# Cross-attention and a gated low-rank layer on one core: q rotated between the two halves of the maxima, k turned behind the gated z

## The chip, the cores and the metric

The kernel runs on one core of one Trainium2 chip. The metric is the time of one execution on the device, in microseconds (us), taken as the median of several runs. Three runs of the kernel before gave 176.37, 176.38 and 176.39 us.

## What is computed

1024 tokens (16 batches of 64) with 512 numbers each go through two layers with residuals.

```
x = x + xattn(layernorm(x), ctx, ctx, position_ids, Wq, Wk, Wv, Wo)
    q = x Wq (32 heads of 16),  k = ctx Wk,  v = ctx Wv (8 heads of 16, each shared by 4 of q)
    q = q*cos + rotate_half(q)*sin,  k the same
    out = softmax(q k^T / 4) v Wo
x = x + ffn(layernorm(x), A, B, Wq_w, keys)
    gate = softmax over the 16 largest of 64 scores, 0 for the others
    z = x A^T (64 experts of rank 8),  out = (z * gate) B^T * 2
```

## The kernel before

The tokens are worked off in T = 8 tiles of 128 rows. Each of the five engines has its own program, written out by hand; the order of the calls in it is the order of execution, and semaphores join the engines. Nothing is planned by a scheduler.

The middle of the program is `step(i)` for i = 1 to 5, and each step works on four tiles at different stages: the attention of tile i is finished (`turned_scores`, `values`, `project_out`); for n = i + 1 the plain scores are formed, their maxima taken and turned; for p = i + 2 the projections of k, v and q are made and rotated; and from i = 2 on (the code calls this `f >= 0`) tile f = i - 2 goes through the gated layer (`project_down`, `turn_zg`, `up_high`, `up_low`). Before the steps stand `first` and `second`, behind them `last`.

Names and lines that matter here:

- TensorE (PE) multiplies in single precision by three products of parts, high by high, high by low and low by high. `product` (L1044 to L1046) does it for q, chunk by chunk; `high_part` (L1051, L1052) and `low_part` (L1056) for the other projections. `turn` (L1064) transposes a tile in four pieces; `turn_k` (L1085) transposes the rotated k in one piece, `turn_m` (L1120) the maxima in two. `scores` is L1111, `values` L1147, `turned_scores` L1130 and L1136.
- VectorE (DVE): `top(n, 0)` and `top(n, 1)` (L771, two reductions each) take the maxima of the scores of both halves of tile n from the PSUM banks of `ps_s`; `rotate_k(p)` (L730, L732, L737) makes k_r; `rotate_q(p)` (L752 q_a, L754 q_b) reads the q that PE has just projected out of the bank `ps_w0`; `k_low(p)` (L743) splits the turned k, `m_parts(n)` (L781, L783) the maxima, `z_low(f)` (L895) the turned gated z. `residual` is L812, `result` L902.
- GpSimd (POOL): `k_blocks(p, 0)` and `(p, 1)` (L304), then `rotated_q(p)` (L294, q_r = q_a + q_b), then `c_low` (L288). ScalarE (ACT): `k_high` (L478), `z_high` (L549), `o_high` (L507).

What ties the engines around the change:

- `rotate_q(p)` waits on DVE for `q_ps`, which PE signals with the last matmul of `project_q(p, [3])`.
- `up_high(f)` writes the bank `ps_w0` too. PE therefore waits in front of it until `q_rot` says that both halves of `rotate_q(p)` have read the projected q.
- `turn_k(p)` waits on PE for k_r of `rotate_k(p)`. Its output goes on to ACT (`k_high`), DVE (`k_low`) and POOL (`k_blocks`).
- `turn_m(n)` waits for `k_low(p)`, since both transposes use one bank, and for `m_parts(n)`; `up_low(f)` waits for `z_low(f)`.

The wait in front of `up_high`, as PE's `step` has it:

```
pe.wait_ge(v_st_ok, p + 1)
project_out(i)
if f >= 0:
    pe.wait_ge(q_rot, 2 * p + 2)
    up_high(f)
```

Of the kernel before, what the change touches and what calls it, by code (L numbers as in the profile page):

```python
# [51 lines left out]
def build(nc, x, cT, pos, wq, wkv, wo, aT, router, bT, out):  # L52
    ctx = ExitStack()
    with ctx:
# [643 lines left out]
        def _(dve):  # L698
# [5 lines left out]
            def statistics1(t):  # L704
                dve.wait_ge(ld_x[t], 16)
                dve.bn_stats(bn1[:], x_sb[:, t % XN, :]).then_inc(stat1, 1)
                dve.wait_ge(stat1, 3 * t + 1)
                if t >= 2:
                    dve.wait_ge(shift1_ok, t - 1)
                else:  # L710
                    dve.wait_ge(xh_ok, 1)
                dve.bn_aggr(mv1[:], bn1[:]).then_inc(stat1, 1)
                dve.wait_ge(stat1, 3 * t + 2)
                dve.tensor_scalar_add(ve1[:], mv1[:, 1:2], EPS).then_inc(stat1, 1)

            def x_low(t):
                dve.wait_ge(x_hi_ok, t - RAW + 1)
                dve.tensor_tensor(xT_lo[:], xhT_bank(t)[:].rearrange("p (k q) -> p k q", k=DK),
                                  xT_hi[:].bitcast(F32), ALU.subtract).then_inc(x_lo_ok, 1)

            def table(at, t, n):
                return cs[:, t, at:at + HD].rearrange("p (s j) -> p s j", s=2).unsqueeze(1)\
                    .broadcast_to([P, n, 2, J])
# [22 lines left out]
            def rotate_q(t):  # L746
                H = REP * KVH
                dve.wait_ge(q_ps, t + 1)
                if t >= 1:
                    dve.wait_ge(q_r_ok, t)  # L750
                w = ps_w0[:].rearrange("p (h s j) -> p h s j", h=H, s=2)
                dve.tensor_tensor(q_a[:].rearrange("p (h s j) -> p h s j", h=H, s=2), w,  # L752
                                  table(0, t, H), ALU.mult).then_inc(q_rot, 1)
                dve.tensor_tensor(q_b[:].rearrange("p (h s j) -> p h s j", h=H, s=2), w[:, :, ::-1, :],  # L754
                                  table(HD, t, H), ALU.mult).then_inc(q_rot, 1)

            def q_low(t):
                dve.wait_ge(qT_hi_ok, t + 1)
                dve.tensor_tensor(qT_lo[:, t % 2].rearrange("p b r q -> p r b q"),
                                  ps_t0[:].rearrange("p (r b q) -> p r b q", r=REP, b=2),  # L760
                                  qT_hi[:, t % 2].bitcast(F32).rearrange("p b r q -> p r b q"),
                                  ALU.subtract).then_inc(qT_lo_ok, 1)

            def top(t, b):
                dve.wait_ge(s_ps, 2 * t + b + 1)
                if t >= 1 and b == 0:
                    dve.wait_ge(m_lo_ok, t)
                for half in range(2):
                    if b == 0 and half == 1:
                        dve.wait_ge(max_ok, 4 * t + 1)  # L770
                    dve.tensor_reduce(neg_top[:, b, HALF_H * half:HALF_H * (half + 1), :],  # L771
                                      ps_s[:, 2 * (1 - b) + half, :].rearrange("p (r h k) -> p h r k", r=2, h=HALF_H),
                                      AX.X, ALU.max, negate=True).then_inc(max_ok, 1)
# [12 lines left out]
            def attend(t, meanwhile=lambda: None):  # L786
                n = 3 * t
                dve.wait_ge(o_ps, t + 1)
                dve.transpose(o_s[:].rearrange("p h u g d -> p (h u g d)"),  # L789
                              ps_o.rearrange("p h n -> p (h n)")).then_inc(o_step, 1)  # L790
                meanwhile()
                dve.wait_ge(o_step, n + 1)
                for h in range(2):
                    mm = dve.reciprocal(inv[:, h, :], o_s[:, h, :, 1 - h, 0])
                mm.then_inc(o_step, 1)
                dve.wait_ge(o_step, n + 2)
                for h in range(2):
                    mm = dve.tensor_tensor(o_t[:, :, h, :], o_s[:, h, :, h, :],
                                           inv[:, h, :].unsqueeze(2).broadcast_to([P, HD, HD]), ALU.mult)
                mm.then_inc(o_step, 1)  # L800
                dve.wait_ge(o_step, n + 3)
                if t >= 1:
                    dve.wait_ge(oT_lo_ok, t)
                dve.transpose(o_n[:], o_t[:].rearrange("p u g d -> p (u g d)")).then_inc(o_ok, 1)  # L804
# [24 lines left out]
            def x2_low(t):  # L829
                hi, lo = x2T_of(t)  # L830
                dve.wait_ge(x2T_hi_ok, t + 1)
                dve.tensor_tensor(lo[:], x2T_bank(t)[:].rearrange("p (k q) -> p k q", k=DK),  # L832
                                  hi[:].bitcast(F32), ALU.subtract).then_inc(x2T_lo_ok, 1)
# [143 lines left out]
            def step(i):  # L977
                f, g, n, p = i - 2, i - 1, i + 1, i + 2
                if p > RAW:
                    x_low(p)  # L980
                if p + 1 < T:
                    statistics1(p + 1)
                if f >= 0:
                    route(f)
                    x2_low(g)
                attend(i, lambda: q_low(n))
                rotate_k(p)
                if f < 0:
                    x2_low(g)
                top(n, 0)  # L990
                top(n, 1)
                k_low(p)
                if f < 0:
                    m_parts(n)
                rotate_q(p)
                if f >= 0:
                    m_parts(n)
                    z_low(f)
                residual(i)
                statistics2(i)  # L1000
                if f >= 0:
                    result(f)
# [38 lines left out]
        def _(pe):  # L1041
# [41 lines left out]
            def turn_k(t):  # L1083
                pe.wait_ge(k_rot, 3 * t + 3)
                pe.transpose(kT_bank(t), k_r[:], ident[:]).then_inc(kT_ps, 1)  # L1085

            def project_q(t, chunks):
                if t == RAW:
                    pe.wait_ge(wq_l, DK)
                pe.wait_ge(x_hi_ok, t - RAW + 1)  # L1090
                pe.wait_ge(x_lo_ok, t - RAW + 1)
                return product(ps_w0[:], chunk(xT_hi), chunk(xT_lo), wq_hi, wq_lo, slice(0, D), chunks)
# [92 lines left out]
            def turn_zg(t):  # L1185
                pe.wait_ge(zg_ok, t + 1 if t < T - 1 else T + 1)
                turn(ps_t1, zg, DK).then_inc(zT_ps, 1)
# [82 lines left out]
            def step(i):  # L1270
                f, g, n, p = i - 2, i - 1, i + 1, i + 2
                turned_scores(i)
                if f >= 0:
                    pe.wait_ge(x2_ok, i)
                    project_down(f, 0)
                    if f >= 1:
                        pe.wait_ge(res_ok, f)
                    else:
                        pe.wait_ge(q_rot, 2 * p)
                    project_q(p, [0, 1])  # L1280
                    pe.wait_ge(z_ok, 2 * f + 1)
                    project_down(f, 1)
                    turn_x2(g)
                else:
                    pe.wait_ge(q_rot, 2 * p)
                    project_q(p, [0, 1, 2])
                values(i)
                turn_q(n)
                if f < 0:
                    pe.wait_ge(mT_ok, n)  # L1290
                    turn_x2(g)
                if f >= 0:
                    pe.wait_ge(z_ok, 2 * f + 2)
                else:
                    pe.wait_ge(x2_ok, i)
                project_kv(p)
                if f >= 0:
                    project_q(p, [2])
                scores(n, 0)
                scores(n, 1)  # L1300
                if f >= 0:
                    pe.wait_ge(x2T_lo_ok, i)
                    turn_zg(f)
                project_q(p, [3]).then_inc(q_ps, 1)
                turn_k(p)
                pe.wait_ge(v_st_ok, p + 1)
                project_out(i)
                if f >= 0:
                    pe.wait_ge(q_rot, 2 * p + 2)
                    up_high(f)  # L1310
                pe.wait_ge(kT_lo_ok, p + 1)
                turn_m(n)
                if f >= 0:
                    up_low(f)
                if p + 1 < T:
                    if f < 0:
                        pe.wait_ge(x2T_lo_ok, i)
                    turn_xh(p + 1)
# [106 lines left out]
```

## Time and profile before

| | us |
|---|---|
| median of three runs | 176.38 (176.37 to 176.39) |
| the profiled execution's own time | 176.11 |
| its span, first to last instruction | 174.4 |
| PE busy | 168.5 (97% of the span) |
| DVE busy | 132.6 (76%) |
| ACT busy | 90.3 (52%) |
| POOL busy | 85.7 (49%) |

A row of the timeline gives the start and the duration of an instruction (or of several, merged, with their count) in us from the start of the span, then engine, line, operation and its output<-inputs; in brackets stands how long the engine had been idle before it and who ended the idle time. "PE" is the matmul itself, "PEld" the load of its stationary operand, which can run beside the matmul before. Matmuls overlap, so two starts in a row tell more than a duration. The mean granted clock of PE is 1.000 of full speed.

### The profile page before, as it was taken

The page shows a single profiled execution, that of the slowest core. Times are in us where ns is not written, and L with a number is a line of the kernel's source. Part 1 is how long each engine was busy: PE and PEld are TensorE (multiplying, and loading weights), DVE is VectorE, ACT ScalarE, POOL GpSimd, SP SyncE. Part 2 cuts the span into 40 slices and gives each one's busy share as a digit, 9 for nine tenths or more (in the row PEclk, how much of TensorE's full clock was granted, in tenths as well). Part 3 has the DMA queues.
Part 4 walks back from the last instruction along what each step waited for, and adds up shares of the span by engine and source line. Part 5 has one row for each costly group of instructions (what it writes and reads, how often), then busy time and mean ns, then how long its engine had stood idle before and what let it go on. Part 6 is the DMA issues. An engine that isn't in the chain of part 4 may idle for free.

```text
span 174.4 us, 4057 instructions
## 1 busy us (share of the span) xinstructions
PE 168.5 (97%) x1440; PEld 130.3 (75%) x1440; DVE 132.6 (76%) x391; ACT 90.3 (52%) x206; POOL 85.7 (49%) x109
## 2 busy tenths in 40 slices
PE   7999999999989999999999999999999999999994
PEld 2555574677869887888779887888879676889883
DVE  1758857987999899749986699549983998758651
ACT  3578899756468325652647326652527335324210
POOL 5499989599559929122761328103630302421100
DMA  5999911002202020101101000100001001000013
GB/s 169 304 400 389 402 35 62 0 6 60 60 4 60 0 64 0 62 4 29 37 0 60 4 0 0 60 6 0 4 0 60 4 0 60 4 4 0 0 60 120
DMA packets 5332, 11.30 MB, mean 65 GB/s; under 512 B 689, under 2 KB 945, under 8 KB 5057
## 3 DMA queue, kind: packets, MB, share of 16 engines
q1 hardware_dynamic: 5024, 10.79, 17.8%
q10 hardware_dynamic: 288, 0.27, 0.5%
q8 instruction: 11, 0.18, 0.4%
q14 instruction: 9, 0.07, 0.1%
HBM read 8.95 MB, written 2.10 MB: 63 GB/s over the span
## 4 chain that ended last, share of the span: by engine, by line
PE 78%; DVE 8%; ACT 4%; POOL 3%; issue 3%; DMA 2%; ACTq 0%; DVEq 0%
PE ps_w L1051 13%; PE ps_w L1052 12%; PE ps_w L1056 11%; PE ps_t L1064 8%; PE ps_s L1111 6%; PE ps_s L1147 5%; PE ps_s L1130 4%; PE ps_w L1044 3%; PE ps_w L1045 3%; PE ps_w L1046 3%; PE ps_s L1052 2%; PE ps_s L1051 2%; PE ps_s L1056 2%; DMA pos_sb<-pos 2%; POOL wkv_lo L271 2%
## 5 line engine op out<-in xcount | busy, mean ns | idle before, releaser
L313 POOL TENSOR_TENSOR oT_lo<-o_n,oT_hi 128x512 fp32r<-128x512 f32 x8 | 10.3, 1291 | 30.5 <-ACT oT_hi L507 30.5
L771 DVE TENSOR_REDUCE ps_s<-ps_s 128x8 f32<-128x512 f32 x32 | 20.7, 692 | 0.9 <-PE ps_s L1111 0.7
L499 ACT ACTIVATE eT<-ps_s 128x512 f32<-128x512 f32 x32 | 17.0, 599 | 4.1 <-PE ps_s L1136 4.0
L328 POOL TENSOR_TENSOR late<-late,gate 128x512 f32<-128x512 f32 x7 | 7.6, 1082 | 22.2 <-DVE gate L864 22.2
L1051 PE MATMUL ps_w<-am_hi,x2T_hi 128*128 128x288 f32 x48 | 13.9, 312 | 0.0
L1052 PE MATMUL ps_w<-am_lo,x2T_hi 128*128 128x288 f32 x48 | 13.2, 297 | 0.0
L1051 PE MATMUL ps_w<-wo_hi,oT_hi 128*128 128x512 f32 x28 | 11.7, 418 | 0.4 <-ACT oT_hi L507 0.4
L1212 PE MATMUL ps_w<-wq_sb,xT_raw 128*128 128x512 f32 x24 | 11.8, 606 | 0.0
L789 DVE STREAM_TRANSPOSE o_s<-ps_s 128x1024 f32<-128x1024 f32 x8 | 10.0, 1244 | 1.8 <-PE ps_s L1147 1.8
L1051 PE MATMUL ps_w<-b_hi,zT_hi 128*128 128x512 f32 (+1 forms) x28 | 11.2, 406 | 0.0
L507 ACT ACTIVATE oT_hi<-o_n 128x512 fp32r<-128x512 f32 x8 | 5.1, 632 | 11.9 <-DVE o_n L804 11.9
L1052 PE MATMUL ps_w<-wo_lo,oT_hi 128*128 128x512 f32 x28 | 11.1, 396 | 0.0
L1052 PE MATMUL ps_w<-b_lo,zT_hi 128*128 128x512 f32 (+1 forms) x28 | 10.5, 379 | 0.0
L832 DVE TENSOR_TENSOR x2T_lo<-ps_t,x2T_hi 128x512 fp32r<-128x512 f32 x7 | 4.8, 690 | 7.4 <-ACT x2T_hi L520 7.4
L1111 PE MATMUL ps_s<-k_bd_hi,qT_hi 64*128 64x256 f32 x64 | 10.1, 311 | 0.0
L1051 PEld LDWEIGHTS ps_w<-am_hi,x2T_hi 128*128 128x128 f32 x48 | 9.0, 188 | 1.4 <-issue 0.2
L294 POOL TENSOR_TENSOR q_r<-q_a,q_b 128x512 f32<-128x512 f32 x7 | 9.1, 1297 | 2.0 <-DVE q_b L754 2.0
L492 ACT ACTIVATE mT<-ps_t 128x256 fp32r<-128x256 f32 x8 | 3.1, 383 | 13.1 <-PE ps_t L1120 13.1
L304 POOL TENSOR_TENSOR k_bd_lo<-kT_lo,half_mask 128x512 fp32r<-128x512 f32 x8 | 8.8, 1095 | 1.9 <-DVE kT_lo L743 1.9
L1111 PEld LDWEIGHTS ps_s<-k_bd_hi,qT_hi 64*128 64x128 f32 x64 | 6.1, 186 | 4.5 <-issue 4.3
L1111 PE MATMUL ps_s<-k_bd_lo,qT_hi 64*128 64x256 f32 x64 | 9.1, 279 | 0.0
L1111 PE MATMUL ps_s<-k_bd_hi,qT_lo 64*128 64x256 f32 x64 | 9.1, 278 | 0.0
(211 smaller groups left out, 524.6 us busy)
## 6 DMA issues: line engine op xcount, KB each, us to landing
x_sb<-x SPq DMA_DIRECT2D x8, 256.0 KB, 7.4
cT_in<-cT SPq DMA_DIRECT2D x7, 256.0 KB, 3.7
out<-res SPq DMA_DIRECT2D x7, 256.0 KB, 2.0
wq_sb<-wq SPq DMA_DIRECT2D x4, 256.0 KB, 6.4
late<-wo SPq DMA_DIRECT2D x1, 1024.0 KB, 8.6
am_sb<-aT SPq DMA_DIRECT2D x1, 1024.0 KB, 8.8
b_sb<-bT SPq DMA_DIRECT2D x1, 1024.0 KB, 7.4
wkv_sb<-wkv SPq DMA_DIRECT2D x1, 512.0 KB, 4.4
```

The lines of the kernel that those rows point to most:

```text
L294: pool.tensor_tensor(q_r[:].rearrange("p (r k d) -> p k r d", r=REP, k=KVH), q_a[:].rearrange("p (k r d) -> p k r d", r=REP, k=KVH), q_b[: ...
L304: pool.tensor_tensor(bd[:, t % 2], kT[:].bitcast(F32).rearrange("p (b q) -> p b q", b=2).unsqueeze(2) .broadcast_to([P, 2, HALF_H, BATCH]) ...
L313: pool.tensor_tensor(oT_lo[:], o_n[:].rearrange("p (b r q) -> p r b q", b=2, r=REP), oT_hi[:].bitcast(F32), ALU.subtract).then_inc(oT_lo_o ...
L499: act.activation(eT[:, c].rearrange("p b n -> p (b n)"), ps_s[:, c, :], ACT.Exp)\
L771: dve.tensor_reduce(neg_top[:, b, HALF_H * half:HALF_H * (half + 1), :], ps_s[:, 2 * (1 - b) + half, :].rearrange("p (r h k) -> p h r k", ...
L789: dve.transpose(o_s[:].rearrange("p h u g d -> p (h u g d)"), ps_o.rearrange("p h n -> p (h n)")).then_inc(o_step, 1)
L1051: pe.matmul(dst, hi(k), w_hi[:, k, cols], start=(k == 0), stop=False)
L1052: pe.matmul(dst, hi(k), w_lo[:, k, cols], start=False, stop=False)
L1056: mm = pe.matmul(dst, lo(k), w_hi[:, k, cols], start=False, stop=(k == DK - 1))
L1064: mm = pe.transpose(dst[:, P * k:P * (k + 1)], src[:, P * k:P * (k + 1)], ident[:])
L1111: mm = pe.matmul(ps_s[:, 2 * (1 - b) + half, 2 * P * rp:2 * P * (rp + 1)], q[rows, t % 2, b, 2 * rp:2 * rp + 2, :].rearrange("p r q -> p ( ...
L1212: return pe.matmul(ps_w0[:], xT_raw[:, k, :], wq_sb[:, k, :], start=(k == 0), stop=(k == DK - 1))
```

## The change

It moves two calls, in the steps with f >= 0 (i = 2 to 5) alone. On DVE `rotate_q(p)` goes from behind `top(n, 1)` and `k_low(p)` to between `top(n, 0)` and `top(n, 1)`. On PE `turn_k(p)` goes from behind `project_q(p, [3])` to directly behind `turn_zg(f)`, ahead of `project_q(p, [3])`. Step 1, and everything before and behind the steps, keeps its order. Nothing is added or removed, and no wait changes.

```diff
@@ DVE, step(i) @@
                 top(n, 0)
+                if f >= 0:
+                    rotate_q(p)
                 top(n, 1)
                 k_low(p)
                 if f < 0:
                     m_parts(n)
-                rotate_q(p)
-                if f >= 0:
+                    rotate_q(p)
+                else:
                     m_parts(n)
                     z_low(f)
                 residual(i)
@@ PE, step(i) @@
                 if f >= 0:
                     pe.wait_ge(x2T_lo_ok, i)
                     turn_zg(f)
+                    turn_k(p)
                 project_q(p, [3]).then_inc(q_ps, 1)
-                turn_k(p)
+                if f < 0:
+                    turn_k(p)
                 pe.wait_ge(v_st_ok, p + 1)
                 project_out(i)
```

DVE, from the end of `rotate_k(p)` to `m_parts(n)` in one step (four steps have this difference; `kT_lo` is `k_low`, `q_a` and `q_b` are `rotate_q`, the reductions are `top`):

```order
 L737 TENSOR_TENSOR k_r<-ps_w,k_b 128x128
-L771 TENSOR_REDUCE ps_s<-ps_s 128x8 x4
-L743 TENSOR_TENSOR kT_lo<-ps_t,kT_hi 128x128
-L752 TENSOR_TENSOR q_a<-ps_w,cs 128x512
-L754 TENSOR_TENSOR q_b<-ps_w,cs 128x512
+L771 TENSOR_REDUCE ps_s<-ps_s 128x8 x2
+L752 TENSOR_TENSOR q_a<-ps_w,cs 128x512
+L754 TENSOR_TENSOR q_b<-ps_w,cs 128x512
+L771 TENSOR_REDUCE ps_s<-ps_s 128x8 x2
+L743 TENSOR_TENSOR kT_lo<-ps_t,kT_hi 128x128
```

The rotation of q has passed two reductions and `k_low`; those three now stand behind it, and `m_parts` follows at the same place in the sequence.

PE, from the transposes of the gated z to the first matmuls of `project_out`, in a step with f >= 0, before:

```order
L1064 MATMUL ps_t<-ident,late 128x128 x4
L1044 MATMUL ps_w<-wq_hi,xT_hi 128x512
L1045 MATMUL ps_w<-wq_lo,xT_hi 128x512
L1046 MATMUL ps_w<-wq_hi,xT_lo 128x512
L1085 MATMUL ps_t<-ident,k_r 128x128
L1051 MATMUL ps_w<-wo_hi,oT_hi 128x512
L1052 MATMUL ps_w<-wo_lo,oT_hi 128x512
```

and changed, where each of PE's line numbers is two higher because of the two lines that DVE's part has gained:

```order
L1066 MATMUL ps_t<-ident,late 128x128 x4
L1087 MATMUL ps_t<-ident,k_r 128x128
L1046 MATMUL ps_w<-wq_hi,xT_hi 128x512
L1047 MATMUL ps_w<-wq_lo,xT_hi 128x512
L1048 MATMUL ps_w<-wq_hi,xT_lo 128x512
L1053 MATMUL ps_w<-wo_hi,oT_hi 128x512
L1054 MATMUL ps_w<-wo_lo,oT_hi 128x512
```

The transpose of k has passed the three matmuls of the last chunk of q. The text uses the line numbers of the kernel before.

## Rows read from the trace of the kernel before

**Rows 1.** Waits over the whole span, PE's and two of DVE's: total, times, longest
```profile
DVE x2T_lo L832 <- ACT x2T_hi L520: 7.4, 5, 2.5
...
PEld ps_w L1051 <- DVE q_b L754: 1.8, 4, 0.4
...
PE ps_t L1120 <- DVE m_split L783: 0.6, 1, 0.6
...
DVE res L902 <- PE ps_w L1056: 1.8, 4, 0.5
```

**Rows 2.** Busy time by stretch, steps 3 and 4: length, each engine, PEclk
```profile
71.51:91.19 19.68, 19.67 (x181) 16.15 (x181) 15.82 (x48) 10.05 (x23) 8.32 (x9) 1.00 0.10 29
91.19:110.87 19.68, 19.68 (x182) 16.15 (x181) 15.83 (x48) 10.06 (x23) 8.31 (x9) 1.00 0.04 14
```

**Rows 3.** Timeline of step 3, where `project_out` ends and `up_high` begins
```profile
86.21 0.89 PEld L1056 LDWEIGHTS ps_w<-wo_hi,oT_lo 128*128 128x128 f32 x4
86.44 1.10 PE L1056 MATMUL ps_w<-wo_hi,oT_lo 128*128 128x512 f32 x4
86.80 0.68 DVE L754 TENSOR_TENSOR q_b<-ps_w,cs 128x512 f32<-128x512 f32 x1
87.54 0.19 PEld L1051 LDWEIGHTS ps_w<-b_hi,zT_hi 128*128 128x128 f32 x1 [0.44 <-DVE q_b L754]
87.54 0.50 PE L1051 MATMUL ps_w<-b_hi,zT_hi 128*128 128x512 f32 x1
87.88 0.40 PE L1052 MATMUL ps_w<-b_lo,zT_hi 128*128 128x512 f32 x1
88.12 0.40 PE L1051 MATMUL ps_w<-b_hi,zT_hi 128*128 128x512 f32 x1
```

**Rows 4.** Timeline in `last`: `project_out` ends, another projection follows without a wait
```profile
148.69 1.09 PE L1056 MATMUL ps_w<-wo_hi,oT_lo 128*128 128x512 f32 x4
149.62 0.29 PE L1051 MATMUL ps_s<-am_hi,x2T_hi 128*128 128x288 f32 x1
```

**Rows 5.** Timeline of step 3, PE around `turn_zg` and `turn_k`
```profile
83.25 0.66 PE L1064 MATMUL ps_t<-ident,late 128*128 128x128 f32 x4
83.66 0.48 PE L1044 MATMUL ps_w<-wq_hi,xT_hi 128*128 128x512 f32 x1
83.99 0.40 PE L1045 MATMUL ps_w<-wq_lo,xT_hi 128*128 128x512 f32 x1
84.22 0.39 PE L1046 MATMUL ps_w<-wq_hi,xT_lo 128*128 128x512 f32 x1
84.45 0.27 PE L1085 MATMUL ps_t<-ident,k_r 128*128 128x128 f32 x1
84.48 0.48 PE L1051 MATMUL ps_w<-wo_hi,oT_hi 128*128 128x512 f32 x1
84.80 0.40 PE L1052 MATMUL ps_w<-wo_lo,oT_hi 128*128 128x512 f32 x1
```

**Rows 6.** Timeline of step 3, DVE from `rotate_k` to `residual`
```profile
83.27 0.29 DVE L737 TENSOR_TENSOR k_r<-ps_w,k_b 128x128 f32<-128x128 f32 x1
83.48 2.62 DVE L771 TENSOR_REDUCE ps_s<-ps_s 128x8 f32<-128x512 f32 x4
...
84.81 0.69 DVE L771 TENSOR_REDUCE ps_s<-ps_s 128x8 f32<-128x512 f32 x1
...
86.01 0.28 DVE L743 TENSOR_TENSOR kT_lo<-ps_t,kT_hi 128x128 fp32r<-128x128 f32 x1
...
86.21 0.68 DVE L752 TENSOR_TENSOR q_a<-ps_w,cs 128x512 f32<-128x512 f32 x1
...
87.72 0.29 DVE L783 TENSOR_TENSOR m_split<-ps_s,m_split 128x128 fp32r<-128x128 f32 x1
...
87.93 0.68 DVE L895 TENSOR_TENSOR zT_lo<-ps_t,zT_hi 128x512 fp32r<-128x512 f32 x1
```

**Rows 7.** Timeline of step 3, its end: PE's `turn_m` and `up_low`, DVE's `result`
```profile
89.51 0.38 PE L1120 MATMUL ps_t<-ident,m_split 128*128 128x128 f32 x2
...
89.65 1.17 PE L1056 MATMUL ps_w<-b_hi,zT_lo 128*128 128x512 f32 x4
...
90.25 0.15 DVE L827 TENSOR_SCALAR ve<-mv 128x1 f32<-128x1 f32 x1
...
90.86 0.69 DVE L902 TENSOR_TENSOR res<-ps_w,late 128x512 f32<-128x512 f32 x1 [0.45 <-PE ps_w L1056]
```

**Rows 8.** POOL's q_r in step 5, and PE's transposes of it in `last`
```profile
126.92 1.31 POOL L294 TENSOR_TENSOR q_r<-q_a,q_b 128x512 f32<-128x512 f32 x1 [0.16 <-DVE q_b L754]
...
132.94 0.60 PE L1064 MATMUL ps_t<-ident,q_r 128*128 128x128 f32 x4
```

**Rows 9.** Timeline of step 3: what else `project_out` and `up_high` wait for
```profile
83.61 1.29 POOL L313 TENSOR_TENSOR oT_lo<-o_n,oT_hi 128x512 fp32r<-128x512 f32 x1 [3.91 <-ACT oT_hi L507]
...
84.93 0.59 ACT L549 ACTIVATE zT_hi<-ps_t 128x512 fp32r<-128x512 f32 x1
```

## The prediction, on record before the run

> **What bounds the kernel now.** I read the busy shares first, then the waits, then the timeline of one step. PE is busy for 97% of the span. In steps 3 and 4 it is busy for all of their 19.68 us, at the full granted clock, while DVE has about 3.9 us to spare [rows 2]. So the steps are PE's, and an edit that moves no work between engines can gain only what PE loses at a seam. Busy time hides such losses, because the durations overlap and the profile stretches a matmul over a short stall. The list of waits shows them: PE's weight load for `up_high` waits for DVE's q_b four times, 1.8 us in all, once in each step with f >= 0 [rows 1]. That is the wait for the bank in which `rotate_q` reads q. The timeline of step 3 shows it at work: q_b ends at 86.80 + 0.68 = 87.48, and the load starts at 87.54, with no weights fetched beside the matmul before it [rows 3].
>
> **What that wait costs.** Not the 0.44 us of idle weight loading. What counts is the distance of matmul starts. With the wait it is 87.88 - 86.44 = 1.44 us from the first L1056 of `project_out` to the second matmul of `up_high` [rows 3]. Where another projection follows `project_out` without a wait, the four L1056 take 149.62 - 148.69 = 0.93 us [rows 4], and a matmul of 512 columns follows its forerunner by 88.12 - 87.88 = 0.24 us [rows 3], so the clean distance is 1.17 us. The wait costs 1.44 - 1.17 = 0.27 us. The other three steps show the same pattern.
>
> **Part one, the rotation of q moved.** q_a may begin when two reductions are done and q is projected. The third reduction starts at 84.81 today [rows 6], so DVE is free for q_a at about 84.81. The projected q is due from PE: its last matmul starts at 84.22 and ends at 84.61 [rows 5]; part two puts a transpose of 0.10 us ahead of it, which gives 84.71. From a PE end to the DVE start that it releases the trace has 89.65 + 1.17 = 90.82 to 90.86 [rows 7], so 0.04 us, and q is visible at 84.75. That is 0.06 us before DVE wants it. q_a and q_b then take 87.48 - 86.21 = 1.27 us as today [rows 3, 6] and end at 84.81 + 1.27 = 86.08. PE would like to fetch the weights of `up_high` a matmul ahead of its clean start at 86.44 + 0.93 = 87.37, at about 87.14. So q_b is some 1.06 us early and the wait is gone. Gain: 0.27 us per step.
>
> What stands behind the rotation gets later. `k_low` moves from 86.01 to 86.01 + 1.27 = 87.28 and ends at 87.56. The rest of DVE's sequence keeps its start, since the same instructions stand ahead of it: the maxima's parts are ready at 88.01 and zT_lo at 88.61 [rows 6]. PE's `turn_m`, which needs `k_low` and the maxima's parts, starts at 89.51 today [rows 7] and at 89.24 with the gain, 1.2 us after them; `up_low` moves from 89.65 to 89.38, 0.77 us after zT_lo. Both are covered. DVE is done with its statistics at 90.40 and waits for PE with `result` until 90.86 [rows 7]; with PE 0.27 us earlier it waits 0.19 us instead of 0.45. Still PE's.
>
> POOL works in order: the low block of k waits for `k_low` and so starts about 1.3 us later, and q_r and the low part of c move with it. In step 5, q_r ends at 126.92 + 1.31 = 128.23 and PE turns it at 132.94 [rows 8]; 1.3 us later still leaves over 3 us. In the other steps the same transpose comes in the next step, further away. These delays cost nothing. If that cover were gone, each would be worth up to 1.3 us.
>
> **Part two, k turned behind the gated z.** PE issues the same transpose at another place. Alone behind the q chunk it costs (84.80 - 84.22) - 2 x 0.235 = 0.11 us, counting the slow start of the matmul behind it; 0.235 because undisturbed starts lie 0.23 or 0.24 apart [rows 3, 5]. As the fifth of a run it costs one more spacing, (83.66 - 83.25) / 4 = 0.10 us [rows 5]. The difference is 0.01 us a step, and I take nothing. The good bound is that the slow exit from the lone transpose (84.80 - 84.48 = 0.32 against 0.235, so 0.09 us) is saved in full and the fifth transpose of the run adds nothing: 4 x 0.09 = 0.36 us. The bad one is a wait: k_r ends at 83.27 + 0.29 = 83.56 [rows 6], and the transpose would start at 83.66. With the 0.06 us from q_b's end to the load behind it [rows 3], k_r is visible at 83.62; the margin is 0.04 us, and if the weight load is held, up to 0.1 us more is lost in a step, 0.4 us in all. A slip of the last q chunk by that much would also make DVE wait by 0.1 us, inside its slack. I take zero, because both ends are small and the exact times say that it just fits.
>
> The Trainium skill, in "TensorE: Matmul & The Clock Gate", section "Back-to-back issue gap", gives about 81 ns per matmul for a sustained stream of weight loads and matmuls of 128 columns. By that the fifth transpose would cost 0.08 us instead of 0.10, and the sum would gain 4 x 0.02 = 0.08 us more. The row here says 0.10.
>
> ACT gets the turned k about 0.8 us sooner, and with it zT_hi, both used later than they are ready. No DMA is moved.
>
> **The sum.** 4 x 0.27 = 1.08 us off, nothing added. The profiled execution's own time is 176.11 us and its span 174.4; they would become 175.03 and 173.3. The median of the runs lies 0.27 us above the profiled one, so I forecast 176.38 - 1.08 = **175.30 us**. `last` waits only for work that the steps before it hand over, so it moves forward as a whole.
>
> **The rivals.** About 0.2% (0.35 us) is what a measurement of this kernel can tell from no change.
>
> *Also the transposes pay.* The lone transpose's slow exit is saved fully: 1.08 + 0.36 = 1.44 us, so 174.94. For it: two exits in rows 5 cost 0.09 each, and one of them disappears. Against it: the single transpose itself shows almost no spacing of its own (84.45 to 84.48), so the exit is the price that it has today. Chance 0.12.
>
> *DVE held by q.* `rotate_q` now waits for the last chunk of q with two reductions, `k_low`, `m_parts` and `z_low` behind it. Were the chunk late by more than the 0.77 us that `up_low` has in hand, PE would wait there instead and the gain would shrink towards nothing. At 0.77 + 0.27 = 1.04 us the time would be today's, 176.4. Against it stands that the chunk comes 0.06 us early and that PE and DVE start this stretch from the same event, the values of tile i. Chance 0.07, with the case that another wait takes the place of q_b's at `up_high`; oT_lo (ready at 84.90) and zT_hi (85.52) are both over 1 us early [rows 9].
> The same page of the Trainium skill says, in the section on the 16 small arrays, that VectorE works off its queue in strict order while TensorE may fetch weights ahead. By that rule nothing behind `rotate_q` can pass it; the trace here has no case with `rotate_q` in this place.
>
> *PE held by k, slower than before.* The transpose of k now stands in front of the last q chunk and of `project_out`. If k_r came later than today relative to PE, PE would stand still. The point from which it decides is 0.04 us of margin plus the 0.27 us gained. If one more operation of 128x512 got ahead of k_r on DVE (0.59 us, q_a to q_b), PE would lose 0.55 us and gain 0.27: 4 x 0.28 = 1.1 us more, 177.5. Against it: nothing on DVE ahead of `rotate_k` has changed, and DVE idles for x2T_hi ahead of the attention, 7.4 us in five times [rows 1], so no delay is carried over. Chance 0.04.
>
> *It does nothing that can be measured*, since small losses of k's wait and the reduction order eat most of the gain. That needs 0.73 us of losses; the bounds above give 0.4. Chance 0.03.
>
> **Chances and range.** My forecast, 175.3 with its own bounds of 174.9 to 175.7, has 0.74. Faster by over 0.2%: 0.74 + 0.12 = 0.86. Within 0.2%: most of the DVE case and the last, 0.09. Slower: 0.05. The range goes from just under the transposes' case, 174.85, to the bad bound of k's wait (175.30 + 0.4 = 175.7) and a little into the shrunken gains, 175.95.
>
> **What would show it.** Right: PE's wait for q_b is missing from the waits, the distance from the first L1056 of `project_out` to the second matmul of `up_high` is 1.17 us in the four steps, a step takes 19.4 us instead of 19.68, the low block of k starts some 1.3 us later, and DVE has no wait before q_a over 0.1 us. Wrong: a wait of PE for k_r before the transpose, a wait of DVE for the projected q that reaches `z_low`, a new wait of PE at `turn_m` or `up_low`, or a longer `last`.

## The result, and the profile after

The changed kernel takes 175.18 us in the median of nine runs, beside 176.32 us for the kernel before. The ratio, taken over all runs and not from the two medians (their quotient is 0.9935), is 0.9945, with a 95% interval of 0.9924 to 0.9966: 0.34% to 0.76% faster. The forecast was 175.30. Two further sets of runs of the same kernel, beside the kernel before on the same chip, gave 175.13 us (ratio 0.9928, 0.9906 to 0.9950) and 175.25 us (0.9934, 0.9913 to 0.9955).

| | before | after |
|---|---|---|
| median | 176.32 us | 175.18 us |
| span of the profiled execution | 174.4 us | 173.3 us |
| its own time | 176.11 us | 174.97 us |
| PE busy | 168.5 us | 167.6 us |
| DVE busy | 132.6 us | 132.6 us |

First the waits. These are whole-span rows of the changed kernel (total, times, longest). PE's line numbers are two higher than before.

```profile
POOL k_bd_lo L304 <- DVE kT_lo L743: 7.7, 5, 1.7
...
DVE res L902 <- PE ps_w L1058: 0.7, 4, 0.2
...
PE ps_t L1122 <- DVE m_split L783: 0.6, 1, 0.6
```

PE's wait for q_b [rows 1] is no longer in the list, and no wait of PE in the steps has come in its place. The wait of DVE's `result` for PE has shrunk from 1.8 to 0.7 us: with PE earlier, DVE's slack there is nearly used up. POOL now waits for the late `k_low`.

The stretches from one start of `turned_scores` to the next, for steps 3 and 4 of the changed kernel, answer to [rows 2]:

```profile
71.16:90.56 19.40, 19.40 (x180) 16.25 (x179) 15.82 (x48) 10.05 (x23) 8.21 (x10) 1.00 0.09 30
90.56:109.97 19.41, 19.41 (x181) 16.27 (x180) 15.83 (x48) 10.06 (x23) 8.23 (x10) 1.00 0.04 14
```

A step has gone from 19.68 to 19.40 us. The seam between `project_out` and `up_high` in step 3, in the changed kernel's timeline, answers to [rows 3]:

```profile
85.06 0.68 DVE L754 TENSOR_TENSOR q_b<-ps_w,cs 128x512 f32<-128x512 f32 x1
...
86.06 1.09 PE L1058 MATMUL ps_w<-wo_hi,oT_lo 128*128 128x512 f32 x4
86.77 0.19 PEld L1053 LDWEIGHTS ps_w<-b_hi,zT_hi 128*128 128x128 f32 x1
...
87.00 0.40 PE L1053 MATMUL ps_w<-b_hi,zT_hi 128*128 128x512 f32 x1
...
87.23 0.40 PE L1054 MATMUL ps_w<-b_lo,zT_hi 128*128 128x512 f32 x1
```

q_b ends at 85.74, and PE fetches the weights of `up_high` at 86.77, 0.23 us ahead of their matmul at 87.00. From the first low matmul of `project_out` to the second of `up_high` it is 87.23 - 86.06 = 1.17 us, where it was 1.44.

PE around the moved transpose, in the same timeline, answers to [rows 5]:

```profile
82.90 0.66 PE L1066 MATMUL ps_t<-ident,late 128*128 128x128 f32 x4
...
82.93 0.29 DVE L737 TENSOR_TENSOR k_r<-ps_w,k_b 128x128 f32<-128x128 f32 x1
...
83.28 0.14 PEld L1087 LDWEIGHTS ps_t<-ident,k_r 128*128 128x128 f32 x1
83.39 0.27 PE L1087 MATMUL ps_t<-ident,k_r 128*128 128x128 f32 x1
...
83.42 0.48 PE L1046 MATMUL ps_w<-wq_hi,xT_hi 128*128 128x512 f32 x1
...
84.20 0.40 PE L1053 MATMUL ps_w<-wo_hi,oT_hi 128*128 128x512 f32 x1
...
84.43 0.39 PE L1054 MATMUL ps_w<-wo_lo,oT_hi 128*128 128x512 f32 x1
```

From the first transpose to the second matmul of `project_out` it is 1.53 us, where it was 84.80 - 83.25 = 1.55. The rows show why so little comes of it. The fifth transpose of the run costs 0.11 us: from the first transpose to the q chunk it is 83.42 - 82.90 = 0.52 us, where it was 83.66 - 83.25 = 0.41. What the lone transpose had cost behind the chunk is saved: 0.03 us to the first matmul of `project_out` (84.45 to 84.48), and the slow exit, 0.32 us between the first two matmuls of `project_out` and now 0.23. The other three steps with f >= 0 show the same. The weights of the transpose, which are k_r, are loaded 0.06 us after k_r's end (83.22 to 83.28), as soon as a load followed q_b's end in [rows 3]. DVE's part answers to [rows 6]:

```profile
83.14 1.42 DVE L771 TENSOR_REDUCE ps_s<-ps_s 128x8 f32<-128x512 f32 x2
...
84.47 0.68 DVE L752 TENSOR_TENSOR q_a<-ps_w,cs 128x512 f32<-128x512 f32 x1
...
86.86 0.28 DVE L743 TENSOR_TENSOR kT_lo<-ps_t,kT_hi 128x128 fp32r<-128x128 f32 x1
...
87.37 0.29 DVE L783 TENSOR_TENSOR m_split<-ps_s,m_split 128x128 fp32r<-128x128 f32 x1
...
87.58 0.68 DVE L895 TENSOR_TENSOR zT_lo<-ps_t,zT_hi 128x512 fp32r<-128x512 f32 x1
```

q_a starts 1.33 us after the first reduction, just where the third reduction stood before (84.81 - 83.48 = 1.33), with no wait for the projected q. The maxima's parts and zT_lo keep their distance from the first reduction (4.23 us for the start of m_split's second operation, 4.24 before).

Where the time came from: `turned_scores` of step 2 starts at 51.85 us before and 51.75 after, that of tile 6 in `last` at 130.09 and 128.93. The four stretches between take 78.24 and 77.18 us, 1.06 less. What follows takes 44.31 and 44.37 us, so `last` has moved forward as a whole.

### The profile page after: what moved, and what is told of

It reads as the page before. It is cut to its first block, busy times and chain, and to the rows that moved or that the text cites. A ratio compares the mean times of both kernels' runs of the same rounds, so it can differ in the third digit from the quotient of the medians.

```text
span 173.3 us, 4057 instructions
## 1 busy us (share of the span) xinstructions
PE 167.6 (97%) x1440; PEld 130.9 (76%) x1440; DVE 132.6 (77%) x391; ACT 90.3 (52%) x206; POOL 85.2 (49%) x109
## 4 chain that ended last, share of the span: by engine, by line
PE 86%; DVE 7%; ACT 3%; issue 2%; ACTq 0%; DVEq 0%
PE ps_w L1053 13%; PE ps_w L1054 12%; PE ps_w L1058 12%; PE ps_t L1066 9%; PE ps_s L1113 6%; PE ps_s L1149 5%; PE ps_s L1132 4%; PE ps_w L1206 3%; PE ps_w L1214 3%; PE ps_t L1071 3%; PE ps_w L1046 3%; PE ps_w L1047 3%; PE ps_w L1048 3%; PE ps_s L1054 2%; PE ps_s L1053 2%
## 5 line engine op out<-in xcount | busy, mean ns | idle before, releaser
L1054 PEld LDWEIGHTS ps_w<-am_lo,x2T_hi 128*128 128x128 f32 x48 | 9.0, 188 | 0.0
```

What stands on the lines that cost most here:

```text
L1054: pe.matmul(dst, hi(k), w_lo[:, k, cols], start=False, stop=False)
```

## The experiments

All measures of a stretch below are from the start of `turned_scores` in one step to that in the next, read from each kernel's timeline. The spans of the traces differ in other places too. `turned_scores` of step 1 starts anywhere from 37.59 us (the changed kernel) to 38.35 us (a kernel below that has the same order up to there), and one of the three traces of the changed kernel takes 1.2 us more behind the steps than the other two. So the stretches tell more than the spans. Over the four of them the three traces of the changed kernel make 77.18, 77.16 and 77.17 us.

**Rotation of q alone.** The changed kernel, with PE's order as before:

```diff
                     turn_zg(f)
-                    turn_k(p)
                 project_q(p, [3]).then_inc(q_ps, 1)
-                if f < 0:
-                    turn_k(p)
+                turn_k(p)
```

> The rotation of q moved alone; k is turned behind the last q chunk as before. My theory: the whole gain is the wait of PE for q_b that goes away, so 176.3 - 1.08 = 175.2 us, with at most 0.1 us lost because the lone transpose of k keeps its slow exit; distance from the first low matmul of project_out to the second matmul of up_high 1.17 us in four steps, step 19.41 to 19.44 us. Rival (the transposes pay a good part): 175.2 + 0.3 = 175.5 or more. Rival (both moves are needed together, since k's turn blocks something): over 175.7.

Measured: 175.40 us, ratio 0.9937 (0.9912 to 0.9961). The stretches of steps 2 to 5 are 19.38, 19.40, 19.40 and 18.96 us, 77.14 together against 77.18 of the changed kernel. The seam in step 3:

```profile
86.53 1.10 PE L1058 MATMUL ps_w<-wo_hi,oT_lo 128*128 128x512 f32 x4
87.47 0.40 PE L1053 MATMUL ps_w<-b_hi,zT_hi 128*128 128x512 f32 x1
87.70 0.40 PE L1054 MATMUL ps_w<-b_lo,zT_hi 128*128 128x512 f32 x1
```

The distance is 1.17 us. The rotation carries the whole gain, and the second move isn't needed for it.

**k turned early alone.** The kernel before, with PE's part of the change:

```diff
                     turn_zg(f)
+                    turn_k(p)
                 project_q(p, [3]).then_inc(q_ps, 1)
-                turn_k(p)
+                if f < 0:
+                    turn_k(p)
```

> k turned directly behind the gated z alone; the rotation of q stays behind both maxima. My theory: PE still waits for q_b at up_high, and q_b's time is set by DVE's own sequence, so what the transpose saves on PE goes into a longer wait: 176.3 us, no change, step 19.66 to 19.68 us, and the wait for q_b still there four times, at 0.44 us or 0.02 more each. The low block of k is not later. Rival (the transposes pay): 175.9 to 176.0. Rival (the turned k, reaching ACT and POOL earlier, helps someone): under 176.1.

Measured: 176.51 us, ratio 1.0004 (0.9978 to 1.0030). The four stretches are 19.68, 19.69, 19.68 and 19.26, 78.31 us together against 78.24 before. In step 3 PE still waits, by a little more:

```profile
87.88 0.19 PEld L1051 LDWEIGHTS ps_w<-b_hi,zT_hi 128*128 128x128 f32 x1 [0.47 <-DVE q_b L754]
```

So this half of the change is worth nothing by itself. The rival in which the transposes pay falls with the two kernels together: with the wait gone, k early or late makes 0.04 us in four steps, in favour of late, and that is hardly more than the 0.02 us by which the changed kernel's three traces differ.

**q rotated ahead of both halves of the maxima.** The changed kernel with:

```diff
-                top(n, 0)
                 if f >= 0:
                     rotate_q(p)
+                top(n, 0)
                 top(n, 1)
```

> The changed kernel with the rotation of q one place earlier still, ahead of both maxima. DVE is free for it at 83.14 us in step 3, but the projected q is visible only at about 84.42, so DVE stands for 1.28 us and everything behind slips by 1.28. My theory of the slack: zT_lo would end at 88.26 + 1.29 = 89.55 against a weight load of up_low wanted at 88.97, the maxima's parts at 88.95 against 88.63; PE loses 0.6 to 0.7 us in each of four steps: 175.2 + 2.6 = 177.8 us, so slower than the kernel before. Rival (DVE's slack is larger than I count, or PE bounds regardless): 175.2 to 175.5. Rival (the loss adds up with another wait, as the next step's inputs come late too): over 179.

Measured: 177.81 us, ratio 1.0095 (1.0059 to 1.0130), slower than the kernel before. The stretches are 19.98, 20.00, 20.00 and 19.56 us: 0.6 us more than in the changed kernel, in each. DVE in step 3, and behind it PE's weight loads for `turn_m` and `up_low`:

```profile
85.27 0.69 DVE L752 TENSOR_TENSOR q_a<-ps_w,cs 128x512 f32<-128x512 f32 x1 [1.18 <-PE ps_w L1048]
...
89.52 0.29 DVE L783 TENSOR_TENSOR m_split<-ps_s,m_split 128x128 fp32r<-128x128 f32 x1
89.73 0.68 DVE L895 TENSOR_TENSOR zT_lo<-ps_t,zT_hi 128x512 fp32r<-128x512 f32 x1
```

```profile
89.93 0.20 PEld L1122 LDWEIGHTS ps_t<-ident,m_split 128*128 128x128 f32 x2 [0.46 <-issue]
90.46 0.77 PEld L1058 LDWEIGHTS ps_w<-b_hi,zT_lo 128*128 128x128 f32 x4 [0.33 <-DVE zT_lo L895]
```

DVE stands for 1.18 us for the projected q, and half of it comes out at `turn_m` and `up_low`. The load for `up_low` starts 0.05 us after zT_lo's end (90.41). For the load of `turn_m` the profile names no releaser, but it starts 0.12 us after the maxima's parts end (89.81). DVE does hold all that is behind `rotate_q`: this is the rival of DVE held by q, made to happen.

**q rotated behind one reduction.** The first reduction of `top(n, 0)` is done, then `rotate_q(p)`, then its second:

```diff
-            def top(t, b):
+            def top(t, b, between=lambda: None):
...
                                       AX.X, ALU.max, negate=True).then_inc(max_ok, 1)
+                    if half == 0:
+                        between()
...
-                top(n, 0)
-                if f >= 0:
-                    rotate_q(p)
+                top(n, 0, (lambda: rotate_q(p)) if f >= 0 else (lambda: None))
                 top(n, 1)
```

> The changed kernel with the rotation of q behind the first reduction of the first half, between the two halves' places of the change and of e3. DVE is free at about 83.8 us in step 3, q visible at 84.42, so DVE stands for 0.6 us in each step. By my count of the slack zT_lo ends at 88.85 against 88.97 wanted and the maxima's parts at 88.25 against 88.63: nothing is lost, 175.2 us, and the only marks are a wait of DVE before q_a of 0.6 us and no wait before result. Rival (any wait of DVE for q is passed on to PE): 175.2 + 4 x 0.6 = 177.6. Rival (part of it): 175.5 to 176.5.

Measured: 175.22 us, ratio 0.9930 (0.9904 to 0.9955). DVE stands for 0.57 us and PE loses nothing:

```profile
84.59 0.69 DVE L752 TENSOR_TENSOR q_a<-ps_w,cs 128x512 f32<-128x512 f32 x1 [0.57 <-PE ps_w L1048]
...
88.31 0.68 DVE L897 TENSOR_TENSOR zT_lo<-ps_t,zT_hi 128x512 fp32r<-128x512 f32 x1
...
90.64 0.15 DVE L829 TENSOR_SCALAR ve<-mv 128x1 f32<-128x1 f32 x1
90.72 0.69 DVE L904 TENSOR_TENSOR res<-ps_w,late 128x512 f32<-128x512 f32 x1
```

```profile
89.17 0.78 PEld L1058 LDWEIGHTS ps_w<-b_hi,zT_lo 128*128 128x128 f32 x4
```

`result` follows its forerunner at once, so DVE's slack in front of it is all used, and the four stretches still make 77.14 us. Between 0.57 and 1.18 us lies the point from which a late q costs time. The rows narrow it: zT_lo ends at 88.99 and PE loads it at 89.17, 0.18 us later, where a load that had to wait followed after 0.05. So some 0.13 us are left, and the point is near 0.57 + 0.13 = 0.70 us. That is an estimate; no run stands there. The prediction counted 0.77, to the start of the matmul and not to the load ahead of it.

**k turned ahead of the gated z.**

```diff
-                    turn_zg(f)
                     turn_k(p)
+                    turn_zg(f)
```

> The changed kernel with k turned ahead of the gated z instead of behind it. k_r ends at 83.22 us in step 3 and the run of transposes begins at 82.90, so PE stands for k_r until about 83.28. My theory: 0.38 us lost in each of four steps, nothing given back, 175.2 + 1.5 = 176.7 us, and q later by 0.38 us, which DVE takes out of its slack. Rival (the wait is hidden by weights fetched ahead): 175.2 to 175.5. Rival (the later q is passed on by DVE to up_low): 177.5 or more.

Measured: 176.95 us, ratio 1.0028 (1.0012 to 1.0044): the gain is more than given back. The stretches are 19.85, 19.85, 19.80 and 19.41 us, 0.45 above the changed kernel's in steps 3 and 5. Step 3:

```profile
83.89 0.30 PE L1087 MATMUL ps_t<-ident,k_r 128*128 128x128 f32 x1 [0.40 <-DVE k_r L737]
```

PE stands for k_r. DVE then waits 0.28 us before q_a and passes nothing on. This is the other rival of the prediction, PE held by k, with its cost shown: 1.73 us for the four stretches (78.91 - 77.18), a little over the 1.5 expected. The transpose starts 0.14 us after k_r's end (83.75), where 0.06 was counted; its weights can't be loaded before k_r is there.

**A repetition and its neighbours around step 1.** The changed kernel was measured twice more:

> The changed kernel once more, unchanged, beside the kernel before on the same chip, as the measure for the other two: 175.2 us, about 1.1 us below the kernel before.

> The changed kernel, unchanged, as the neighbour of the next one on the same chip: 175.15 us.

The numbers stand above (175.13 and 175.25). Beside them stand kernels that try to win more. PE's largest wait left in the middle is in step 1, where the turn of the maxima starts at 50.87, 0.74 us after the matmuls ahead of it allow. The first attempt moved the split of the turned x2 in step 1:

```diff
                 rotate_k(p)
-                if f < 0:
-                    x2_low(g)
                 top(n, 0)
...
                 if f < 0:
                     m_parts(n)
+                    x2_low(g)
                     rotate_q(p)
```

> The changed kernel, with one more move in step 1 alone: the split of the turned x2 on DVE goes from ahead of the maxima to behind their parts. In step 1 PE starts the turn of the maxima 0.74 us later than the matmuls ahead of it allow (49.20 + 0.93 = 50.13 to 50.87), since DVE's sequence is late. My theory: the maxima's parts come 0.59 us sooner, the turn of the normalised x then waits for the split instead (about 50.8 against 51.12 today), and 0.3 to 0.35 us is left of it: 174.85 us. Rival (the wait only moves to the split): 175.2. Rival (the late split of x2 holds the next step's first projection): slower, 175.5.

Measured: 175.04 us, ratio 0.9924 (0.9903 to 0.9944), not to be told from the changed kernel. Step 1 takes 13.77 us instead of 14.17, and step 2 takes 19.72 instead of 19.40, so most of what step 1 gains is lost again in step 2. The next kernel tried to keep the 0.4 us:

```diff
+                m_parts(n)
                 if f < 0:
-                    m_parts(n)
+                    x2_low(g)
+                    residual(i)
                     rotate_q(p)
                 else:
-                    m_parts(n)
                     z_low(f)
-                residual(i)
-                statistics2(i)
+                    residual(i)
+                    statistics2(i)
...
                 if p > RAW:
                     x_low(p)
+                if f == 0:
+                    statistics2(g)
```

(with the move of `x2_low` as above)

> The changed kernel with DVE's order changed around step 1 alone. In the trace of the late split of x2 the 0.38 us won at the turn of the maxima is lost again in step 2, where PE waits for xT_lo, which stands behind the statistics of x2 (about 1.0 us). Here the split of x2 stays behind the maxima's parts, the residual goes ahead of the rotation of q, and the statistics go behind xT_lo. My theory: xT_lo ends about 0.9 us sooner, nothing on PE waits for it, and the 0.3 to 0.4 us of step 1 are kept: 174.8 us, with 0.3 us less from the start of step 1's turn of the maxima to the start of step 3. Rival (DVE is full from the attention of step 1 to the middle of step 2, so any order pays its work somewhere): 175.1.

Measured: 175.52 us, ratio 0.9950 (0.9930 to 0.9970). Step 1 takes 13.78 us, but step 2 takes 19.93. POOL, DVE and PE in step 2:

```profile
57.00 1.28 POOL L271 TENSOR_TENSOR b_lo<-b_sb,b_hi 128x512 fp32r<-128x512 f32 x1
```

```profile
57.06 1.31 DVE L854 SCALAR_TENSOR_TENSOR e_top<-s_b,e_sb 128x64 f32<-128x64 f32 x1
...
64.13 0.29 DVE L737 TENSOR_TENSOR k_r<-ps_w,k_b 128x128 f32<-128x128 f32 x1
```

```profile
64.47 0.14 PEld L1088 LDWEIGHTS ps_t<-ident,k_r 128*128 128x128 f32 x1 [0.42 <-DVE k_r L737]
```

DVE's L854 takes 0.23 us in the later steps and 0.51 in step 2 of the changed kernel. Here it starts just behind the start of POOL's split of b (57.00 to 58.28) and ends at 58.37. k_r comes 0.6 us late (12.34 us behind the start of `turned_scores`, where it is 11.76 in the changed kernel's third trace), and PE stands for it in front of the last q chunk: the rival of k once more, this time by itself. Two kernels took it apart. One puts k behind the q chunk again:

```diff
                     turn_zg(f)
-                    turn_k(p)
                 project_q(p, [3]).then_inc(q_ps, 1)
-                if f < 0:
-                    turn_k(p)
+                turn_k(p)
```

> The kernel of the step 1 edits, with k turned behind the last q chunk again, as before the change. In that kernel's trace step 1 gained 0.39 us (14.17 to 13.78) and step 2 lost 0.53 (19.40 to 19.93), because DVE's operation of L854, which reads two tiles of SBUF, ends only when POOL's split of b does (58.37 against 58.26; 1.31 us instead of 0.23), and k_r comes 0.6 us late to a transpose that stands in front of the last q chunk. My theory: with the transpose behind that chunk PE does not wait for k_r; 0.1 us for the late qT_lo stays: 174.9 us, step 2 at 19.5 us, L854 still at 1.3 us once. Rival (DVE's delay reaches PE in another place): 175.3 to 175.5.

The other rotates q ahead of the residual in step 1, so that POOL's operations start sooner:

```diff
                     x2_low(g)
-                    residual(i)
                     rotate_q(p)
+                    residual(i)
```

> The kernel of the step 1 edits, k turned early as in the change, but in step 1 q is rotated ahead of the residual, so that POOL's q_r, cT_lo and b_lo begin 1.2 us sooner, at the times that they had in the changed kernel. If DVE's L854 is held by POOL's tensor operation in flight, it meets the same boundary as in the changed kernel: 0.5 us instead of 1.3, k_r is in time, no wait of PE at the transpose of k, and the gain of step 1 is kept but for 0.1 us at the first projection of step 2, which waits for the residual: 174.85 us, step 2 at 19.5 us. Rival (the hold has nothing to do with POOL but with the operation's own inputs): L854 stays at 1.3 us and the time at 175.5.

Measured: 175.70 us (ratio 0.9939, 0.9906 to 0.9972) and 175.61 us (0.9936, 0.9905 to 0.9967), beside a kernel before that took 176.84 in this set. Both times miss their forecasts, 174.9 and 174.85, also when the slower set is allowed for. The traces say more. With k behind the chunk, step 2 takes 19.49 us as expected, though L854 is held as long:

```profile
57.38 1.32 DVE L854 SCALAR_TENSOR_TENSOR e_top<-s_b,e_sb 128x64 f32<-128x64 f32 x1
```

With q ahead of the residual L854 is back at 0.5 us, as it should be if POOL is the cause. It starts at the same 57.06, now inside a split of POOL that ends at 57.50, and ends at 57.58, ahead of the bulk of the next split:

```profile
56.19 1.31 POOL L271 TENSOR_TENSOR b_lo<-b_sb,b_hi 128x512 fp32r<-128x512 f32 x1
...
57.06 0.52 DVE L854 SCALAR_TENSOR_TENSOR e_top<-s_b,e_sb 128x64 f32<-128x64 f32 x1
...
57.43 1.31 POOL L271 TENSOR_TENSOR b_lo<-b_sb,b_hi 128x512 fp32r<-128x512 f32 x1
```

But step 2 takes 19.72 us, not the 19.5 expected, because the residual is late by 0.39 us, ACT's work behind it too, and PE waits for ACT's copy of z:

```profile
PEld ps_w L1054 <- ACT late L531: 0.4, 1, 0.4
```

From `turned_scores` of step 1 to that of tile 6, the kernel with k behind the chunk takes 91.04 us (38.35 to 129.39) and the changed kernel, in its third set, 91.34 (37.98 to 129.32). By the traces it is 0.3 us better; the times, with ratios of 0.9939 and 0.9934 to the kernel before, don't tell them apart. The interval of such a ratio is up to 0.6 us wide to either side, so this doesn't show a better version.

## Why the prediction was right

- **The bound and the wait's price.** The step was PE's, and the wait for q_b cost 0.27 us by the distance of starts, not the 0.44 of the idle weight load. Measured: 1.44 to 1.17 us, four times; 1.06 us over the four stretches against 1.08 forecast. Had the 0.44 been taken, the forecast gain would have been 1.76 us. The medians differ by 1.14 us; the 0.06 us above the forecast are far inside their interval.
- **Part one.** q was to be visible 0.06 us before DVE wants it; DVE has no wait before q_a. `k_low` was put at 1.27 us later relative to DVE's other work; from the first reduction it is 86.86 - 83.14 = 3.72 us against 86.01 - 83.48 = 2.53, so 1.19. The 1.27 is the time from q_a's start to q_b's end; on DVE the next operation starts before the last one's recorded end, and q_a and q_b each take up 0.60 us from start to start. `turn_m`, `up_low` and POOL's later work cost nothing, as said. The 0.19 us that were to be left of `result`'s wait are 0.17 to 0.2.
- **Part two.** Taken as nothing, between a gain of 0.36 and a loss of 0.4 us. Measured over the four steps: 0.04 us lost with the rotation moved, 0.07 without, the latter between single traces. The good bound had the slow exit saved and the fifth transpose free. The exit is saved (0.32 to 0.23 us), but the transpose costs 0.11, so the two cancel, as the taken value has it. That k_r is just in time was also right; no wait for it appears. Part two is not neutral in one respect, which the prediction had only as a rival: it takes PE's margin for k_r from 0.83 us (visible at 83.62 and used at 84.45 before) to 0.11 (83.28 and 83.39 now), and the load of its weights already follows k_r as closely as a load can that had to wait (0.06 us). The kernels around step 1 show the price: 0.44 us in step 2 (19.93 against 19.49) when k_r came 0.6 us late.
- **The rivals.** DVE held by q has its point between 0.57 and 1.18 us; PE held by k costs 0.39 to 0.45 us a step when k is moved one place further. Both are real mechanisms, and neither acts in the change itself. The rule of the Trainium skill ("TensorE: Matmul & The Clock Gate", section on the 16 small arrays), that VectorE takes its queue in strict order, is borne out by the kernel with q ahead of both halves: DVE stands for 1.18 us, and the four reductions behind q_a, the first of which starts right behind k_r in the changed kernel, all wait with it. The fifth transpose was put at 0.08 us by the same page and at 0.10 by the rows; it costs 0.11.

## What to carry to other kernels

When one engine is busy throughout, look for the seams at which it waits for another engine to release a buffer, and price them by the distance of starts against a clean seam of the same kind; busy time and the idle time of the weight load both mislead. Then move the release just far enough forward: here q rotated behind two reductions is in time, behind one it uses most of the slack, and ahead of all four it makes the kernel slower than at the start. A move on the busy engine that shows no gain may still spend its margin for a late input.

## What the runs showed of the hardware

DVE's operation L854 reads two tiles of SBUF, 128 x 64 each, and takes 0.23 us in most steps, 0.5 in step 2 of the kernel before and of the changed one, and 1.31 or 1.32 us in two of the kernels around step 1. In those it started 0.05 or 0.06 us after the start of an instruction of POOL that reads SBUF (57.00 in the row above) and ended 0.08 or 0.09 us after that instruction's end at 58.28. When POOL's instructions were shifted by the order of other work, it took 0.52 us again, and again it ended 0.08 us after the end of the split that was running when it started (57.50). The 0.51 us of the changed kernel's step 2 end in the same way. So a short operation of one engine can wait for the whole of a long one of the other, and the delay shows as a long duration, not as idle time or as a wait.
The Trainium skill states this in "SBUF — State Buffer", sections "SBUF: two separate sides" and "Who interferes with whom": the two engines share one pair of ports, which is locked for a whole instruction when DVE has two inputs in SBUF and GpSimd reads SBUF. The traces agree: the hold of 1.31 us ends with POOL's 1.28 us instruction. The prediction for the change did not need it: the moved operations read q, the turned k or the scores from PSUM and at most one tile of SBUF, and q_a takes 0.68 us in the old place and in the new. The attempt with a forecast of 174.8 us did need it. It missed by 0.7 us, of which the trace puts 0.44 on the hold, by way of the late k_r. The two forecasts made after it, which allowed for the hold, missed by about as much; why their times don't show what their traces gain is open.
